# Attention's x from the third group on: saved to DRAM, read back in 32-row blocks and turned by VectorE; its statistics one tile earlier

## The reference

```
mod = silu(c) @ wmod  ->  sa, ca, ga, sb, cb, gb
h = layernorm(x) * (1 + ca) + sa
qkv = h @ W_qkv + b_qkv          # 16 heads of 32
q = elu(q / sqrt(32)) + 1.0001;  k = elu(k) + 1.0001
num_t = q_t @ sum_(s<=t) k_s v_s^T;  den_t = q_t . sum_(s<=t) k_s + 1e-6
x = x + ga * ((num / den) @ W_out + b_out)
h = layernorm(x) * (1 + cb) + sb
x = x + gb * ((silu(h @ Wg^T) * (h @ Wu^T)) @ Wd^T)
```

## Time and profile before

| | |
|---|---|
| median of 3 runs | 1997.45 us (1996.22 to 1999.36) |
| the profiled execution | 1998.45 us, span 1996.7 us |
| TensorE busy | 1960.6 us, 98% of the span |
| VectorE busy | 1443.1 us, 72% |
| ScalarE, GpSimd busy | 905.7 us, 877.4 us |
| TensorE's granted clock, mean | 0.998 |
| attention's groups 1 to 13 | from 127.11 to 894.77 us |
| one looped group | 59.07 us |

### The profile page before, as it was taken

The page is one execution under the profiler, slowest core; times in us unless marked ns, Lnnn a source line. Parts: engine busy times, 40 slices in busy tenths (PEclk is TensorE's granted clock), DMA queues, the critical chain, the costliest instruction groups (busy, mean ns, idle before and its releaser), DMA issues. The chain is left out here.

```text
span 1996.7 us, 43856 instructions
## 1 busy us (share of the span) xinstructions
PE 1960.6 (98%) x16008; PEld 1591.9 (80%) x16008; DVE 1443.1 (72%) x2386; ACT 905.7 (45%) x1542; POOL 877.4 (44%) x718
## 2 busy tenths in 40 slices
PE   7999999999999999999899999999999999999999
PEld 4788888888888888887678888788888888888887
DVE  7977888878788878787865857658576585765744
ACT  5443444344444434443344535445354453544533
POOL 2533544444544444453334443444434444344444
PEclk9999999999999999999999999999999999999999
DMA  7223333444434434432575654656546565465553
GB/s 268 69 91 102 115 123 119 135 130 133 135 100 133 128 125 135 127 110 90 179 263 176 207 187 145 214 170 209 186 144 215 171 210 186 144 214 174 169 168 106
DMA packets 202521, 309.81 MB, mean 155 GB/s; under 512 B 16145, under 2 KB 72977, under 8 KB 202386
## 3 DMA queue, kind: packets, MB, share of 16 engines
q1 hardware_dynamic: 201858, 306.78, 48.1%
q10 hardware_dynamic: 528, 1.05, 0.1%
HBM read 225.19 MB, written 82.58 MB: 154 GB/s over the span
## 5 line engine op out<-in xcount | busy, mean ns | idle before, releaser
L1497 POOL TENSOR_TENSOR h_lo<-y_rows,h_hi 128x512 fp32r<-128x512 f32 x192 | 246.5, 1301 | 367.6 <-ACT h_hi L1595 367.6
L461 POOL TENSOR_TENSOR x_res<-y,x_res 128x512 f32<-128x512 f32 x64 | 86.6, 1353 | 294.0 <-DVE y L872 283.5
L851 DVE TENSOR_TENSOR probs<-sc,causal 128x512 f32<-128x512 f32 x256 | 158.5, 681 | 3.8 <-PE sc L1156 2.6
L612 ACT ACTIVATE z_exp<-pj,qk_neg 128x512 f32<-128x512 f32 x128 | 87.7, 686 | 161.5 <-PE pj L1137 158.0
L1137 PE MATMUL pj<-xt_hi,w_hi 128*128 128x512 f32 x512 | 145.9, 406 | 5.7 <-DVE a_t L861 4.7
L1925 PE MATMUL sc<-wd,h_hi 128*128 128x512 f32 x384 | 150.7, 392 | 0.0
L1925 PE MATMUL sc<-wd,h_lo 128*128 128x512 f32 x384 | 149.6, 389 | 0.0
L450 POOL TENSOR_TENSOR a_lo<-a_t,a_hi 128x512 fp32r<-128x512 f32 x60 | 82.2, 1370 | 144.8 <-ACT a_hi L626 144.8
L1137 PE MATMUL pj<-xt_lo,w_hi 128*128 128x512 f32 x512 | 138.1, 391 | 1.8 <-DVE xt_lo L789 1.8
L1137 PE MATMUL pj<-xt_hi,w_lo 128*128 128x512 f32 x512 | 138.1, 392 | 0.0
L1710 DVE TENSOR_TENSOR r_den<-pj,k_tok 128x512 f32<-128x512 f32 x96 | 66.3, 691 | 97.9 <-ACT k_tok L1578 52.2
(11 more groups left out here) (248 smaller groups left out, 5390.4 us busy)
## 6 DMA issues: line engine op xcount, KB each, us to landing
w_hi<-parts SPq DMA_DIRECT2D x48, 1024.0 KB, 5.4
w_lo<-parts SPq DMA_DIRECT2D x48, 1024.0 KB, 5.4
x_mid<-x_res SPq DMA_DIRECT2D x96, 256.0 KB, 2.8
x_res<-in_L_attn_x SPq DMA_DIRECT2D x64, 256.0 KB, 2.8
k_dram<-k_block SPq DMA_DIRECT2D x252, 64.0 KB
xg<-in_L_attn_x SPq DMA_DIRECT2D x15, 1024.0 KB, 7.4
x_res<-x_mid SPq DMA_DIRECT2D x60, 256.0 KB, 3.9
full<-x_mid SPq DMA_DIRECT2D x60, 256.0 KB, 3.7
```

The lines of the kernel that those rows point to most:

```text
L461: pool.tensor_tensor(out=x_res[:, slot, :], in0=y[:, :], in1=x_res[:, slot, :], op=ALU.add).then_inc(y_ready, 1)
L612: act.activation(z_exp[:, n % 2, :], pj[:, n % 2, :], ACT.Relu, bias=qk_neg[:, 1 - kind, c:c + 1], scale=-scale).then_inc(below_ready, 1)
L851: dve.tensor_tensor(out=probs[:, h, :].rearrange("p (c i) -> p c i", c=C), in0=sc[:, h, :].rearrange("p (c i) -> p c i", c=C), in1=causal[ ...
L1497: pool.tensor_tensor(out=h_lo[b], in0=h[i], in1=h_hi[b].bitcast(F32), op=ALU.subtract).then_inc(h_lo_ready, 1)
```

## The change

From the third group on, x is no longer turned by TensorE. After `norm_x` SP saves normalized `xg` to a DRAM buffer `x_norm` of 512 x 512 (`save_x`) and reads it back into the same `xg` with four transfers (`load_blocks`), each for 32 partitions: partition i of block h gets the rows i, i+32, ... of columns 128h to 128h+127, in runs of 512 bytes. One VectorE instruction (`turn_x`) then transposes each 32 x 32 square of the 128 x 2048 buffer in place, and `xt_full` reads its quarters from there with strides instead of from PSUM. The rows of the weights and of the modulation are regrouped on the host to fit, and for the first two groups x comes regrouped as an own input, `x_first`, and is turned by TensorE as before; so is the first half of the feed-forward part's first x (turned in group 14).

The order changes with it: in the loop all four statistics and the variance stand in tile 0, ahead of the gate; GpSimd's rstd stands in tile 0 too; normalizing opens tile 1; `load_group` stands ahead of `load_units` and waits for ScalarE (`xf_ready`) instead of TensorE. In group 0 statistics and normalizing stay where they were, and saving, reading back and turning come a tile later than in the loop.

```diff
@@ -302,9 +306,25 @@
 
     def sync(sp, first_loads):
         def load_group(g):
-            wait(sp, xt_ps, C * g)
-            sp.dma_start(xg[:, :, :], x_groups[g, :, :, :] if isinstance(g, int) else
+            if isinstance(g, int) and g < 3:
+                wait(sp, xt_ps, C * g)
+            else:
+                wait(sp, xf_ready, C * g)
+            sp.dma_start(xg[:, :, :], x_first_groups[g, :, :, :] if isinstance(g, int) and g < 2 else
+                         x_groups[g, :, :, :] if isinstance(g, int) else
                          x_groups[bass.ds(g, 1), :, :, :].rearrange("a p t d -> (a p) t d")).then_inc(x_in, 16)
+
+        def save_x(g):
+
+            wait(sp, xn_ready, g + 1)
+            sp.dma_start(x_norm.rearrange("(t p) d -> p t d", p=P), xg[:, :, :]).then_inc(x_saved, 16)
+
+        def load_blocks(g):
+
+            wait(sp, x_saved, g * 16 + (-16))
+            for h in range(HPC):
+                sp.dma_start(xg[h * E:(h + 1) * E, :, :].rearrange("p t (b x) -> p (t b) x", x=P),
+                             x_norm[:, h * P:(h + 1) * P].rearrange("(b i) x -> i b x", i=E)).then_inc(x_blocks_in, 16)
 
         def load_residual(tile, slot, uses):
             wait(sp, y_out[slot], 16 * uses)
@@ -392,20 +412,23 @@
         load_k(0, 0)
 
         def group(g, parity):
-            if not isinstance(g, int):
-                load_units(g, parity)
             if not isinstance(g, int) or g + 2 < NG:
                 load_group(g + 2)
+                if not isinstance(g, int):
+                    load_units(g, parity)
             else:
                 half = g + 2 - NG
                 for slot in range(2):
                     sp.wait_ge(y_out[slot], 16 * GT // 2 * (half + 1))
-                sp.wait_ge(xt_ps, C * (NG + half))
+                sp.wait_ge(*((xf_ready, C * NG), (xt_ps, C * (NG + 1)))[half])
                 sp.dma_start(xg[:, :, :], mid_groups[half, :, :, :]).then_inc(x_in, 16)
             for t in range(GT):
                 tile = g * GT + t
                 if not isinstance(g, int) and t == 3:
                     store_made(g, parity, 1)
+                turned = not isinstance(g, int) or g + 2 < NG
+                if turned and t == 1 and not (isinstance(g, int) and g == 0):
+                    save_x(g + 2)
                 load_residual(tile, t % 2, g * 2 + t // 2)
                 if not isinstance(g, int) or tile + 2 < NG * GT:
                     save_k(*((g, t + 1) if t + 1 < GT else (g + 1, 0)))
@@ -420,6 +443,11 @@
                         sp.dma_start(later.wd[:, j, :].bitcast(F32), downs[j, :, :]).then_inc(wd_in[j // C], 16)
                 if not isinstance(tile, int) or tile > 0:
                     store(tile - 1, (t + 1) % 2)
+                if turned and t == 2 and isinstance(g, int) and g == 0:
+                    save_x(g + 2)
+                    load_blocks(g + 2)
+                if turned and t == 1 and not (isinstance(g, int) and g == 0):
+                    load_blocks(g + 2)
                 if not isinstance(g, int) or tile + 2 < NG * GT:
                     load_k(*((g, t + 1) if t + 1 < GT else (g + 1, 0)))
                 if not isinstance(g, int) and t > 0:
@@ -531,6 +559,8 @@
             last = isinstance(g, int) and g == NG - 1
 
             last_bias(g, 0)
+            if two_ahead and not (isinstance(g, int) and g == 0):
+                rstd_of(g + 2)
             if last:
                 for op in (B11, B21):
                     for k in range(2):
@@ -594,7 +624,11 @@
                 return evacuate(g, c, bank)
             wait(act, xt_ps, g * C + c + 1)
             wait(act, xt_lo_done, g * C + c - 1)
-            act.activation(xf[:, c % 2, :], bank, ACT.Identity, bias=mod_col[:, SA, c:c + 1],
+            to, turned = xf[:, c % 2, :], bank
+            if not isinstance(g, int) or g >= 2:
+                to = to.rearrange("p (b i) -> p b i", i=E)
+                turned = xg[:, :, :].rearrange("p t (b c i) -> p c (t b) i", c=C, i=E)[:, c, :, :]
+            act.activation(to, turned, ACT.Identity, bias=mod_col[:, SA, c:c + 1],
                            scale=mod_col[:, CA, c:c + 1]).then_inc(xf_ready, 1)
 
         def xt_high(g, parity, c):
@@ -699,18 +735,27 @@
 
             exp_relu(n, 5)
             exp_relu(n, 6)
-            xt_full(g + 2, 0, x_bank)
-            xt_high(g + 2, parity, 0)
+            if g_last_turn:
+                xt_full(g + 2, 0, x_bank)
             exp_relu(n, 7)
-            if looped:
-                act.wait_ge(down_out, g * 16 + (-16))
-            xt_full(g + 2, 1, x_bank)
-            xt_high(g + 2, parity, 1)
+            if g_last_turn:
+                xt_full(g + 2, 1, x_bank)
+            elif not at_start:
+                xt_full(g + 2, 0, x_bank)
+                xt_high(g + 2, parity, 0)
+                if looped:
+                    act.wait_ge(down_out, g * 16 + (-16))
+                xt_full(g + 2, 1, x_bank)
+                xt_high(g + 2, parity, 1)
             state_out(g * GT + 2)
             a_high(g * GT + 2)
             if looped:
                 unit_to_float(g, parity, 1)
 
+            if at_start:
+                for c in range(2):
+                    xt_full(g + 2, c, x_bank)
+                    xt_high(g + 2, parity, c)
             xt_full(g + 2, 2, x_bank)
             xt_high(g + 2, parity, 2)
             if looped:
@@ -776,6 +821,12 @@
                                         ALU.subtract, ALU.mult)
             if tiles[-1] == GT - 1:
                 ins.then_inc(xn_ready, 1)
+
+        def turn_x(g):
+
+            wait(dve, x_blocks_in, g * (16 * HPC) + (-16 * HPC))
+            blocks = xg[:, :, :].rearrange("p t d -> p (t d)")
+            dve.transpose(blocks, blocks).then_inc(xt_ps, C)
 
         def a_low(tile):
             dve.wait_ge(a_hi_ready, tile + 1)
@@ -972,27 +1023,33 @@
             near_last = isinstance(g, int) and g == NG - 2
             first = isinstance(g, int) and g == 0
 
+            turned = looped or g + 2 < NG
+
             mask(g * GT)
             if not first:
                 v_rows(g, parity, 3)
+                norm_stats(g + 2)
             if looped:
                 word_size(g, 0, r_den[other][:, 2, :], (unit_in[0], g * 16 + (-16)))
                 word_size(g, 1, r_den[other][:, 1, :], (down_in, g * 16 + (-16)))
             feature(n, other, 0)
+            if not first:
+                norm_var(g + 2)
             spread(g * GT, g, parity, 0)
             feature(n, other, 1)
             k_blocks(g, parity, 1)
             gate_last(g, 0)
-            if not first:
-                norm_stats(g + 2, range(3))
             divide(g * GT, g, parity, 0)
             if near_last:
                 dve.wait_ge(beyond_ps, 1)
                 dve.tensor_scalar(wide[:, :], x_bank[0:1, 0:1], 0.5, None, ALU.is_gt).then_inc(wide_ready, 1)
 
             mask(g * GT + 1)
-            norm_stats(g + 2, range(0 if first else 3, GT))
-            norm_var(g + 2)
+            if first:
+                norm_stats(g + 2)
+                norm_var(g + 2)
+            else:
+                norm_x(g + 2)
             feature(n, other, 2)
             spread(g * GT + 1, g, parity, 1)
             k_blocks(g, parity, 2)
@@ -1000,7 +1057,8 @@
             feature(n, other, 3)
             gate_last(g, 1)
             feature(n, other, 4)
-            norm_x(g + 2)
+            if first:
+                norm_x(g + 2)
             divide(g * GT + 1, g, parity, 1)
 
             mask(g * GT + 2)
@@ -1009,19 +1067,25 @@
             feature(n, other, 5)
             den_of(n, 1)
             feature(n, other, 6)
-            xt_low(g + 2, parity, 0)
+            if turned and not first:
+                turn_x(g + 2)
             feature(n, other, 7)
             gate_last(g, 2)
             divide(g * GT + 2, g, parity, 2)
             den_of(n, 2)
-            xt_low(g + 2, parity, 1)
             if looped:
                 word_size(g, 2, r_den[other][:, 3, :], (unit_in[1], g * 16 + (-16)))
+            if not first:
+                xt_low(g + 2, parity, 0)
 
             mask(g * GT + 3)
             v_rows(n, other, 0)
+            if first:
+                turn_x(g + 2)
+                xt_low(g + 2, parity, 0)
             spread(g * GT + 3, g, parity, 3)
             k_blocks(n, other, 0)
+            xt_low(g + 2, parity, 1)
             den_of(n, 3)
             v_rows(n, other, 1)
             xt_low(g + 2, parity, 2)
@@ -1145,9 +1209,11 @@
             wait(pe, y_gated, min(tile - 1, (NG - 1) * GT - 1) if isinstance(tile, int) else tile - 1)
             if isinstance(tile, int) and tile == (NG - 2) * GT + 1:
                 pe.wait_ge(wide_ready, 1)
-            if not isinstance(g, int) or g + 2 <= NG:
+            if isinstance(g, int) and g == 0:
+                pe.wait_ge(xf_ready, 2 * C)
+            elif isinstance(g, int) and g + 2 == NG:
```

(25 more changed lines are left out.)

23 lines of the change are left out of this document (13 added, 10 removed).

## The result

The changed kernel takes 2104.39 us (median of 4 runs, 2094.22 to 2112.48), the kernel before beside it 1997.39: a ratio of 1.0532, 95% interval 1.0485 to 1.0579. It is slower, as forecast, but by 107 us instead of 22, and outside the range. The profiled execution took 2094.22 us, the shortest of the four, with a span of 2092.5; the one before had 1996.7.

What follows compares the result with a forecast made beforehand. TensorE, 98% busy, was taken as the bound. Twelve looped groups at +1.0 (-2.5 + 2.5 + 1.0), group 0 +8.3, group 1 0, group 14 +1: 21.3 on the profiled 1998.45, median 2019 us, range 1988 to 2045.

Steps and rivals of the forecast that it cites:

- the two places: Looped groups: TensorE's scores wait for gated y, about 2.5 us in tile 1 and 1 us in tile 3.
- Transposes removed, -2.51 a group: Tiles 2 and 3: without transposes all four tiles last 14.14 us, the group 56.56 instead of 59.07.
- Statistics ahead of the gate, stall 2.5: Tile 0: VectorE waits for x, gate ends at 16.6, TensorE ready at 14.14 stands 2.5 us; bounds 0.4 to 4.2.
- x lands at 6.9: Looped tile 0: load of x lands 6.9 us after the tile's scores start, from store, 0.88 issue and 5.6 transfer.
- Read-back and transpose ahead of the gate of tile 2, stall 1.0: Tile 2: VectorE's 2.3 us transpose and the late k load delay the gate; TensorE stands 1.0 us, bounds 0.6 to 4.0.
- it lands near 7.5 into tile 2: The k load queued behind the block reads lands near 7.5 us into tile 2; VectorE reaches its transpose at about 5.5.
- Rival E: Block reads take 8.4 us, not 5.6; tile 2 stall 4.0, 2055 us; sign: longest wait at transpose, for blocks. Chance 0.10.
- I count none in the loop: Looped groups: the 2.5 us stalls bring no fall of TensorE's clock; if every one fell, 12 x 1.7 = 20 us more.
- B: The clock falls in looped groups as well: 2019 + 20 = 2039 us; sign: clock near 0.95 in the loop. Chance 0.17.
- Group 0: Tile 3: VectorE waits for the block reads, numerators late, scores +6.6 us; with the clock fall +8.3.
- Rival D: Tile 0: x is there when VectorE asks, gate hardly late, stalls 0.4 and 0.6; about 1987 us, faster. Chance 0.13.
- C: Looped groups: stalls of 1.8 together instead of 3.5 just eat the gain, about 1998 us. Chance 0.10.

Runs made afterwards that it cites:

- the last run: Both orders mended, group 0's save and reads a tile up, transpose behind the gate; then tile 1's k feature behind its division, tile 2's denominator behind v: 1980.73 us, 0.9908.
- the run with the part alone: Kernel before, transposes kept on TensorE, with statistics and variance ahead of tile 0's gate and x loaded ahead of the weight words: 2044.99 us, 1.0244.
- 2 KB rows: Changed kernel with the four block reads as plain reads in 2 KB rows instead of 512 B, so other data is computed: 2090.15 us, 1.0476.
- TensorE was kept busy: Changed kernel plus ten overwritten 128x512 matmuls ahead of the scores of tiles 1 and 3 in groups 1 to 12: 2068.21 us, 1.0353.
- both orders mended: Changed kernel with statistics and variance behind tile 0's gate, weight words loaded ahead of x, and k loaded ahead of the block reads: 2012.56 us, 1.007.
- the run with the transpose behind the gate: Both orders mended; from group 1, normalization behind tile 1's gate, x transpose behind tile 2's division, dependent transfers and reads moved too: 2002.00 us, 1.0016.
- the run behind the division: Both orders mended, group 0 a tile up, transpose behind the gate; then normalization behind tile 1's division, tile 2's denominator behind tile 3's v: 2049.93 us, 1.0261.

## Why the prediction was wrong

The direction, the two places and the releasers were right. Three sizes were not, and all erred to the same side. In the loop the wait for k was 23 us too small (2.93 - 1.0 in 12 groups) and left out the numerators' 6.5, the clock's 27 were put at nothing, and the wait for x was 9 too small (3.25 - 2.5 in 12). Groups 0, 1 and 14 add 5. These are 71 of the 73 us that the sum of the groups was off.

*Transposes removed, -2.51 a group:* right, by the last run's group 1.

*Statistics ahead of the gate, stall 2.5:* 3.12 measured in group 6, 3.25 in the mean. The step that failed is "x lands at 6.9": in group 6 it is there at 472.27 - 464.03 = 8.2. I took the 0.88 from the store to the load of x from group 1; in the loop it is 466.16 - 464.67 = 1.49, the store comes 0.64 into the tile instead of 0.35, and x lands in 6.1 instead of 5.6. From there to the end of the gate 9.0 went by, not 9.7. So the term was off by 0.6 in group 6 and by 0.75 in the mean, inside its bounds; the run with the part alone shows the wait as well.

*Read-back and transpose ahead of the gate of tile 2, stall 1.0:* 2.9 measured, the stall that was further off. The transpose was right (2.31 against 2.3). What failed is "it lands near 7.5 into tile 2": k was issued at 500.92 and landed 6.0 later, at 506.92 - 497.05 = 9.9 into it. I let the four reads be issued in no time at all (2.0 to 2.6 us on SP, with k behind), and gave k a landing of under 1 us behind the blocks. Rival E had this size of stall, 4.0, but for packets that are slow; with 2 KB rows k was nearly as late, and in the loop VectorE never waited for the blocks at the transpose, the sign named for E.

*The clock, "I count none in the loop":* 15 of 24 waits brought it down, by 1.5 to 2.9 us each where I had 1.7 for a fall; (1.34 + 0.91) x 12 = 27 us, and 36 came back when TensorE was kept busy. The sign named for B, a clock near 0.95 in the loop, is there: 0.96. I judged by one wait of 1.9 that did no harm and one of 2.8 that did; the stalls came out at 3, and one wait of 1.9 was too few to judge by (see the last section). The Trainium skill's page "TensorE: Matmul & The Clock Gate" (HAM oscillation), by which the sum was 2039, was nearer than my reading of the row; the trace bears it out in 15 of the 24 tiles, not in all.

*Rivals as exclusive cases:* B came together with a stall toward E's, since the stalls are what pulls the clock down. With E's stall in the sum, B was no longer a matter of 0.17. Added up, 2019 + 20 + 36 would have been 2075.

*Group 0:* the place and the mechanism were right, +10.3 against +8.3. *Group 1:* +4.2 against 0, as it has the late k and a fall of the clock behind it (its tiles 2 and 3 take 17.66 and 16.85 us). *Group 14:* -0.1 against +1.

*Rival D (faster, x early) and C:* in all 12 looped groups VectorE waited for x at the statistics, 3.5 us in the mean, and the two stalls together are 6.2 us, not C's 1.8. (That no 1 MB load lands in under 5.6 was too strong a reading of two rows: the page before has 5.4 for 48 loads of weight parts.) That the idea itself can win showed only when the order was mended: 17 us below the kernel before, by six edits.

## What to carry to other kernels

An engine with a fifth of its time free, as VectorE here, is not free at a given place: find the result that the busy engine waits for next, and put new work behind it, not ahead of it. Transfers put into an in-order queue delay each one behind them, first by the time of their issue (2.6 us here) and then in its landing (6.0 us instead of 2.8), so a small load that someone waits for goes first. And a stall's price is its length and the clock behind it; when two stalls grow together, their costs belong in one sum, not in two rivals.

## What was not expected of the hardware

Waits of about equal length do not bring the clock down alike: behind 3.12 us it fell, behind 2.96 in the same group it did not, and in the run with both orders mended waits up to 1.7 left the loop at 1.00. Nor is 1.9 a safe length. In group 4 of the run with the transpose behind the gate, the tile behind the one wait for y took 15.74 us, with the clock at 0.50 from 327 to 330 us:

```profile
325.66 1.17 PE L1217 MATMUL sc<-qt,kt 32*128 32x128 f32 x32 [1.91 <-DVE y L918]
...
341.40 1.17 PE L1217 MATMUL sc<-qt,kt 32*128 32x128 f32 x32
```

In the run with one part alone in the kernel before, a wait of 2.54 (group 13) left the tile behind it at 14.14. What decides between them stays open.

Reads in runs of 512 bytes landed in 5.2 us, in rows of 2 KB in 5.0.

Four VectorE normalizations of 128x512 took 1.91 us before, 2.87 in the changed kernel's new place (group 6) and 3.87 in that of the run behind the division (group 2). GpSimd was idle during the first four, busy for 1.67 us of the second and for 2.76 of the third, ScalarE for 0.00, 0.78 and 3.35; whether either is the cause no run shows.
